# Hybrid convolution, attention and feed-forward kernel on Trainium2: the mean of the first feed-forward block's output is taken out by an fp16 matmul where the output is added, in place of an fp32 centring in the norm behind it

## What is computed

```
x = conv_block(x, L0); x = conv_block(x, L1)       # pointwise 24->96, depthwise 3x3, pointwise 96->24, shortcut
t = tokens(x)
t = t + linear_attention(_ln_t(t))
t = t + quantised_ffn(_ln_t(t), L2)                # fp8 products, fp16 sums
t = t + fourier_block(_ln_t(t))                    # FFT over the tokens, scale, ReLU, inverse FFT
t = t + quantised_ffn(_ln_t(t), L3)

def _ln_t(v, eps=1e-05):
    m = jnp.mean(v, axis=-1, keepdims=True)
    s = jnp.var(v, axis=-1, keepdims=True)
    return (v - m) / jnp.sqrt(s + eps)

def _qlinear(x, W, b):
    y = q_acc(jnp.einsum('bsk,nk->bsn', q_mul(x), q_mul(W)))
    return q_acc(y + q_mul(b))
h = jax.nn.relu(_qlinear(x, W1, b1)); y = _qlinear(h, W2, b2)
```

## Time and profile before

| | us |
|---|---|
| median of 3 runs (lowest to highest) | 2623.15 (2612.8 to 2631.39) |
| the profiled execution | 2623.52 |
| its span, first to last instruction | 2621.4 |
| TensorE busy | 2183.9 |
| VectorE busy | 1927.7 |
| ScalarE busy | 1611.5 |
| mean granted TensorE clock, as a share of full speed | 0.874 |

### The profile page before, as it was taken

How to read it: one execution, slowest core, us unless ns; L and a number is a source line. 1 busy time by engine, 2 the same in 40 slices (tenths; PEclk the granted TensorE clock), 3 DMA queues, 4 the chain that set the end, 5 groups by cost and what they waited for, 6 DMA issues and landing times.

```text
span 2621.4 us, 49010 instructions
## 1 busy us (share of the span) xinstructions
PE 2183.9 (83%) x19776; PEld 1269.9 (48%) x19776; DVE 1927.7 (74%) x3744; ACT 1611.5 (61%) x2758; POOL 113.7 (4%) x290
## 2 busy tenths in 40 slices
PE   3677878998889888998889887998889988986865
PEld 1233334663446534664446534465346634662653
DVE  4886987897768795799858795885957988456153
ACT  3344457855677575765777565864867647757554
POOL 1000000000000000000000000000000000000000
PEclk9887989998789898999889896996889988976665
DMA  5001001000020001000010002000010000000000
GB/s 137 1 1 19 1 1 20 2 2 1 1 38 2 1 1 35 4 2 1 4 35 2 2 1 38 1 2 1 1 30 2 2 1 1 20 2 1 20 1 19
DMA packets 108592, 29.69 MB, mean 11 GB/s; under 512 B 104144, under 2 KB 104272, under 8 KB 107984
## 3 DMA queue, kind: packets, MB, share of 16 engines
q1 hardware_dynamic: 108368, 26.56, 5.0%
HBM read 16.91 MB, written 9.63 MB: 10 GB/s over the span
## 4 chain that ended last, share of the span: by engine, by line
DVE 41%; PE 38%; ACT 11%; issue 6%; SPq 3%; DMA 1%; ACTq 0%; DVEq 0%
DVE acc L1475 20%; PE P L745 6%; PE P L726 5%; PE P L945 4%; PE P L1037 3%; SPq L586 3%; DVE SQ L1621 3%; PE P L794 3%; PE P L958 2%; PE P L986 2%; DVE arena L1605 2%; DVE T L1491 2%; PE P L767 1%; DVE T L1635 1%; PE P L1000 1%
## 5 line engine op out<-in xcount | busy, mean ns | idle before, releaser
L1475 DVE SCALAR_TENSOR_TENSOR acc<-H,Dm,acc 128x784 f32<-128x784 f32 x1024 | 989.4, 1027 | 74.1 <-ACT acc L1113 73.6
L726 PE MATMUL P<-T,Wk 112*128 112x448 f32 (+1 forms) x768 | 393.5, 605 | 77.3 <-ACT H L1106 37.7
L745 PE MATMUL P<-H,diag 64*64 64x392 f32 x4608 | 404.6, 501 | 18.4 <-DVE T L1491 18.4
L1106 ACT ACTIVATE H<-P,biasA 128x448 f32<-128x448 f32 (+1 forms) x384 | 236.0, 622 | 250.5 <-PE P L726 159.9
L745 PEld LDWEIGHTS P<-H,diag 64*64 64x64 f32 x4608 | 172.2, 135 | 234.0 <-issue 203.7
L726 PEld LDWEIGHTS P<-T,Wk 112*128 112x128 f32 x768 | 131.5, 203 | 201.5 <-ACT H L1106 103.3
L1136 ACT ACTIVATE acc<-P,biasT 128x392 f32<-128x392 f32 x128 | 68.6, 584 | 185.5 <-PE P L745 185.5
L794 PE MATMUL P<-T,pack_b 112*112 112x448 f32 x224 | 125.1, 655 | 15.0 <-DVE T L1580 7.9
L1491 DVE SCALAR_TENSOR_TENSOR T<-P,bias,T 112x392 f32<-112x392 f32 x128 | 77.2, 621 | 73.0 <-PE P L767 72.7
L970 PE MATMUL P<-pack_b,arena 128*96 128x112 f32 x928 | 111.5, 269 | 22.8 <-DVE roots L1621 11.7
L1113 ACT ACTIVATE acc<-H,Dm 128x784 f32<-128x784 f32 x128 | 121.9, 952 | 13.6 <-PE P L767 11.4
(11 more groups left out here) (205 smaller groups left out, 3766.8 us busy)
## 6 DMA issues: line engine op xcount, KB each, us to landing
xin<-in_x SPq DMA_DIRECT2D x224, 42.0 KB, 2.3
out_y<-arena SPq DMA_DIRECT2D x8, 1176.0 KB, 6.0
pack_b<-in_pack_b SPq DMA_DIRECT2D x1, 3926.5 KB, 18.0
arena<-in_pack_s SPq DMA_DIRECT2D x1, 1584.0 KB, 8.8
pack_a<-in_pack_a SPq DMA_DIRECT2D x1, 1084.0 KB, 5.4
pack_i<-in_pack_i SPq DMA_DIRECT2D x1, 320.0 KB, 3.1
arena<-in_pack_k SPq DMA_DIRECT2D x1, 192.0 KB, 3.3
```

What stands on the lines that cost most here:

```text
L726: pe.matmul(conv_rows(slice(0, 128), HB[(NP * s + e) % len(HB)], n), Wk1[:, 128 * j:128 * (j + 1)], image_rows(T[q % 3], a, n), start=True ...
L745: last = pe.matmul(conv_rows(slice(64 * h, 64 * (h + 1)), CVB + r, HH), diag[64 * r:64 * (r + 1), tap, :], H1[64 * r:64 * (r + 1), slot(s, ...
L1106: act.activation(H1[:, slot(s, j), o:o + n, 1:1 + HW], conv_rows(slice(0, 128), HB[(NP * s + e) % len(HB)], n), ACT.Relu, bias=biasA[:, j, ...
L1475: ins = ve.scalar_tensor_tensor(a, H1[:, slot(s, j), r:r + SR, c:c + HW], Dm[:, j, tap:tap + 1], a, ALU.mult, ALU.add)
```

## The change

In norm 2 the fp32 centring and the copy back are gone; ScalarE squares a chunk as soon as the feed-forward's add of it is done. In the first feed-forward, the biased fp16 output goes through one more matmul, fp16, with a 112 x 112 matrix `cen16` (24 times the centring matrix, so that its entries are whole numbers), into the output bank that the second layer has used; VectorE then adds 1/24 of that PSUM result to T in place of the fp16 tile. The output bank is free for the next chunk after this add, where it was free after ScalarE's copy. The add of chunk c stands one chunk later in the order than its bias. Norm 2 needs no bank, no `cenk` matrix and no semaphores for centring. The bare steps without an instruction that norms 1 and 3 had on TensorE are gone too. All turn strings are written anew (except that the shape of the order is as before: convolutions of quad q beside the middle of q - 1 and the back of q - 2).

```
-        "b3 m4 b3 m4 b1 m2 b2 m3 b2 m1 b176 "
+        "b130 "
...
+        cen16 = sb("cen16", [R, R], F16)
...
+        free_psum = sig("mean_free_ffn_out_in_psum", NCK)
...
-                    yield
-                    if i == 0:
-                        pe.wait_ge(written.sem, written.at(q, 2 * NS + rows_added(c) if n == 0 else c + 1))
+                    if n == 0:
+                        yield
+                        pe.wait_ge(written.sem, written.at(q, 2 * NS + rows_added(c)))
                         if c >= NC:
                             pe.wait_ge(norm.d_ready.sem, norm.d_ready.at(q, c - NC + 1))
-                        pe.matmul(P[0:R, cen[c % NC], 0:CK], par["cen" if n == 0 else "cenk"][0:R, :],
+                        pe.matmul(P[0:R, cen[c % NC], 0:CK], par["cen"][0:R, :],
...
-                        pe.wait_ge(f.out_half.sem, f.out_half.at(q, c - len(ob) + 1))
+                        read = f.added if L == 0 else f.out_half
+                        pe.wait_ge(read.sem, read.at(q, c - len(ob) + 1))
...
+                def mean_free(c):
+                    pe.wait_ge(f.out_biased.sem, f.out_biased.at(q, c + 1))
+                    stand(pe)
+                    pe.matmul(P[0:R, ob[c % len(ob)], 0:CK], cen16[:, :], f.o16[:, 1, c % 2, :],
+                              start=True, stop=True).then_inc(free_psum.sem, 1)
 
                 for c in range(NCK):
                     for j in range(NT):
                         v = NT * c + j
+                        if L == 0 and c >= 2 and j == 1:
+                            yield
+                            mean_free(c - 2)
                         yield
...
+                if L == 0:
+                    yield
+                    mean_free(NCK - 2)
                 yield
                 second(NCK - 1)
+                if L == 0:
+                    yield
+                    mean_free(NCK - 1)
...
-                    if i == 0:
+                    if n == 0:
                         act.wait_ge(norm.cen_psum.sem, norm.cen_psum.at(q, c + 1))
                         act.activation(D, P[0:R, cen[c % NC], 0:CK], ACT.Copy).then_inc(norm.d_ready.sem, 1)
                         act.wait_ge(norm.d_ready.sem, norm.d_ready.at(q, c + 1))
                     elif n == 1:
                         act.wait_ge(at_added.sem, at_added.at(q, c + 1))
+                    elif n == 2:
+                        act.wait_ge(ffns[0].added.sem, ffns[0].added.at(q, c + 1))
...
+                ve.tensor_scalar(cen16[:, :], par["cen"][0:R, :], float(CH), None, ALU.mult)
...
-                def out_add(c):
+                def out_bias(c):
                     ve.wait_ge(f.out_half.sem, f.out_half.at(q, c + 1))
                     ve.tensor_scalar(f.o16[:, 1, c % 2, :], f.o16[:, 0, c % 2, :], qb[L][0:R, NT:NT + 1], None, ALU.add).then_inc(f.out_biased.sem, 1)
-                    ve.wait_ge(f.out_biased.sem, f.out_biased.at(q, c + 1))
+
+                def out_add(c):
                     t = T[q % 3][:, CK * c:CK * (c + 1)]
-                    ve.tensor_tensor(t, t, f.o16[:, 1, c % 2, :], ALU.add).then_inc(f.added.sem, 1)
+                    if L == 0:
+                        ve.wait_ge(free_psum.sem, free_psum.at(q, c + 1))
+                        last = ve.scalar_tensor_tensor(t, P[0:R, ob[c % len(ob)], 0:CK], 1.0 / CH, t, ALU.mult, ALU.add)
+                    else:
+                        ve.wait_ge(f.out_biased.sem, f.out_biased.at(q, c + 1))
+                        last = ve.tensor_tensor(t, t, f.o16[:, 1, c % 2, :], ALU.add)
+                    last.then_inc(f.added.sem, 1)
...
+                    if c >= 2 and L == 0:
+                        yield
+                        out_add(c - 2)
                     if c >= 1:
                         yield
-                        out_add(c - 1)
-                yield
+                        out_bias(c - 1)
+                        if L == 1:
+                            out_add(c - 1)
...
-    c["cenk"] = c["cen"] + np.diag((np.arange(R) >= MR) & (np.arange(R) < PAD))
```

More of the change, by code:

```diff
@@ L74 @@
              ("w1", (NT * 128,)), ("b1", (NT,)), ("w2", (NT, R)), ("b2", (1,)))],
-    "b": [("cen", (R,)), ("cenk", (R,)), ("rest", (RC,)), ("sgn", (1,)), ("selv", (32 + (NCK - 1) * QI,)), ("m97", (RC + 1,)),
+    "b": [("cen", (R,)), ("rest", (RC,)), ("sgn", (1,)), ("selv", (32 + (NCK - 1) * QI,)), ("m97", (RC + 1,)),
           ("s97", (RC,)), ("wva", (CH,)), ("wkbd", (RC,)), ("bk", (1,)), ("wqt", (CH + 1,)),
@@ L86 @@
     "gpsimd": (
-        "d7 b1 c10 m1 c1 m1 c5 m1 c4 b2 c2 m2 c4 b2 c1 m1 c4 b2 m1 c1 m1 c3 b1 c1 b1 m1 c4 b2 c1 m1 c1 m1 c4 "
-        "b2 c1 m1 c4 b2 m1 c1 m1 c4 b2 c2 m1 c3 b2 c1 m2 c4 b2 m1 c3 b1 c1 b1 m1 c2 m1 c4 b2 c1 m1 c3 b2 m3 "
-        "b5 "
[3 rows of a table added]
     ),
     "tensor": (
[46 rows of a table removed]
[47 rows of a table added]
     ),
     "scalar": (
[37 rows of a table removed]
[38 rows of a table added]
     ),
     "vector": (
[23 rows of a table removed]
[30 rows of a table added]
     ),
@@ L474, in build @@
         for half, norm, layers in (("middle", normM, 2), ("back", normB, 2)):
-            norm.cen_psum = sig(f"centered_in_psum_{half}", NCK)
-            norm.d_ready = sig(f"centered_ready_{half}", NCK)
             norm.sq_ready = sig(f"squares_ready_{half}", layers * NCK)
@@ L484, in build @@
             norm.y_ready = sig(f"normalised_ready_{half}", layers * NCK)
+        normM.cen_psum = sig("centered_in_psum", NCK)
+        normM.d_ready = sig("centered_ready", NCK)
+        free_psum = sig("mean_free_ffn_out_in_psum", NCK)
         ones_ready = sig("yt_ones_ready", 2)
@@ L1043, in back @@
             def back(q):
-                yield from layer_norm(q, normB, 2, ffns[0].added)
+                yield from layer_norm(q, normB, 2)
                 yield from fourier(q)
@@ L1573, in ffn @@
                 f = ffns[L]
-                def out_add(c):
+                _, ob = ffn_banks(q, L)
+                def out_bias(c):
                     ve.wait_ge(f.out_half.sem, f.out_half.at(q, c + 1))
                     ve.tensor_scalar(f.o16[:, 1, c % 2, :], f.o16[:, 0, c % 2, :], qb[L][0:R, NT:NT + 1], None, ALU.add).then_inc(f.out_biased.sem, 1)
-                    ve.wait_ge(f.out_biased.sem, f.out_biased.at(q, c + 1))
+                def out_add(c):
                     t = T[q % 3][:, CK * c:CK * (c + 1)]
-                    ve.tensor_tensor(t, t, f.o16[:, 1, c % 2, :], ALU.add).then_inc(f.added.sem, 1)
+                    if L == 0:
[5 more added lines that the diff above has]
+                    last.then_inc(f.added.sem, 1)
                 for c in range(NCK):
@@ L1590, in ffn @@
                     last.then_inc(f.biased.sem, 1)
+                    if c >= 2 and L == 0:
+                        yield
+                        out_add(c - 2)
                     if c >= 1:
                         yield
-                        out_add(c - 1)
+                        out_bias(c - 1)
+                        if L == 1:
+                            out_add(c - 1)
+                if L == 0:
+                    yield
+                    out_add(NCK - 2)
                 yield
+                out_bias(NCK - 1)
+                if L == 0:
+                    yield
                 out_add(NCK - 1)
```

## The result

The changed kernel takes 2444.7 us (median of 4 runs, 2441.9 to 2448.8); the kernel before takes 2619.2 us on the same chip (4 runs). The profiled execution of the changed kernel took 2448.8 us, its span is 2447.0 us, and the mean granted clock rose from 0.874 to 0.903.

The account below looks back on a forecast made before the run. No engine was taken as full; a chain of waits changing engine bounds the kernel. Span 2621.4 - 17 (steady part) - 20 (end) = 2584.4, with 2.1 around it 2586.5, put to the median 2586; stated 2585, range 2565 to 2605.

Parts of the forecast that it names:

- The new orders themselves: All engines' rewritten step lists: may cost or give some 10 us, widening the range; not given a chance as a case.
- the steady part: Quads 0 to 6: 0 to 39 us less, 20 taken, less VectorE's 3 us: 17 us gained.
- the end: Behind the last convolution: quad 7's deviation 14.4 us after quad 6's last add instead of 28.9; 20 us gained (14 to 26).
- The price of a centring: Norm behind the feed-forward: removing centring frees 5.3 us of TensorE and 3.8 us of ScalarE per quad.
- The fp16 pass and the add: First feed-forward: each pass 0.3 us (range 0.19 to 0.35); VectorE's add from PSUM 0.05 us dearer, 3 us in all.
- The gap: Between one quad's convolution and the next, 1300 to 1340 us: 5.6 us of the chain are centring that the change removes.
- The router some 3 us sooner behind the last input piece: Sign of being right, in the gaps between quads: no centring on the chain, so the router's work starts earlier.
- The single output bank: Rival, middle's feed-forward, quads 0 to 6: bank held until the add, 1.4 us more per chunk, 69 us, 2655; chance 0.1.
- The clock: Rival, seven gaps: without dense fp32 passes the lower clock level lasts 10 us longer each, 35 us lost, 2621; chance 0.1.
- Only the end gains: Rival: input loads and the round trip take the gap's freed time; steady part nothing, end 14 us, 2612; chance 0.2.
- more than forecast: Rival: every gap gives its 5.6 us and the end 26 us, 2561; chance 0.12.
- as dear as fp32: Rival, first feed-forward: fp16 matmul costs as much as an fp32 one, so 25 us come back, 2611; chance 0.03.

Follow-up runs that it names:

- fp32_new_order: The kernel before with its fp32 centring and waits kept, but the changed kernel's step orders on all engines: 2482.7 us, ratio 0.947.
- experiment 1: Two kernels against the kernel before: old arithmetic in the new orders, 2482.7 us (0.947); new arithmetic in the old orders, 2726.6 us (1.040).

## Why the prediction was wrong

The step that failed is the sentence "The new orders themselves, which move every step a little, may cost or give some 10 us beside all this; that widens the range and is no case of its own." The orders alone gave 138 us in place of 10. No row stood behind the 10. That the steps move little is so: counted in the lists, 2.4 places in the mean on VectorE and 3.2 on TensorE, at most 27 and 28; that little movement makes little difference was assumed. The trace of the kernel before had what was at stake: VectorE idle for 413 us of the stretch, 147 of them in front of the taps and of the convolutions' output adds. The orders alone took away 109 of the 413 and 89 of the 147, with the same work on VectorE (1928.3 us busy, before 1927.7).

**The forecast for the rest agrees with the arithmetic's measured worth by luck.** Forecast -37, measured -38 on the new orders. It was split as 17 in the steady part and 20 at the end; from `fp32_new_order` to the changed kernel it is 34.9 in the stretch and 3.2 at the end. The forecast's 20 at the end were mainly the new list's, which gave 27.6 there; both together 30.8. So the term for the steady part was half of what was measured, and the term for the end, by its own reasoning mostly order, stands in for the rest.

**The price of a centring.** The forecast counted 5.3 us of TensorE and 3.8 us of ScalarE a quad. Over eight quads that is 73 us of work, of which 45 are seen in the time, 28 and 17.5. In the steady part the change came to 35, near the upper end of 0 to 39. That end was built on 5.6 us in each of seven gaps; but 2.2 of the 5.6 were norm 0's (above), and the gap was the longest of the seven, so that the reading at the gap would have given 7 x 3.4 = 24 at most. The gain lies in other places as well.

**The fp16 pass and the add.** The pass takes 352 ns at least and 368 at the median; 0.3 was taken, from a range to 0.35, so it lies just above that range. The add from PSUM was to be 0.05 us dearer than the one in SBUF and is not: 618 ns against a median of 626. Two lines by source, min/median/max:

```profile
L916 PE MATMUL P<-mid,cen x56: 352/368/622, 373.2 to 2272.7; 112*112 112x448 f16 x56
...
L1614 DVE SCALAR_TENSOR_TENSOR T<-P,T x56: 610/618/626, 377.1 to 2273.4; 112x448 f32<-112x448 f32 x56
```

**The gap.** "The router some 3 us sooner behind the last input piece" is wrong at the gap shown, 15.2 us against 14.5, though the gap is 20 us shorter. **The end.** Quad 6's output matmuls stand where it was forecast; the deviation comes behind quad 6's last add 18.1 us, forecast 14.4, because the last two chunks need 4.7 us from the output matmuls' end to the last add (2269.30 to 2274.0) where one pass and one add were counted.

**The single output bank** was a true mechanism with a price that was too low, and its condition was missing. In orders that were not made for it, it turns the change into a loss: the held bank costs 102/49 = 2.1 us a chunk, over the 0.76 from which it decides and over the 1.4 that was priced (the whole fp16 way 135/49 = 2.8). In the new orders TensorE waits 12.2 us for it in all. Why: the lists put other matmuls between a chunk's hidden layer and the second layer behind it, so that the bank is free, or nearly so, when its turn comes (experiment 1).

**The clock.** As a loss of the changed kernel it is out: 0.874 before, 0.906 with the new orders, 0.903 with the arithmetic as well. How much of the orders' 138 us is the higher clock's (the same instructions keep TensorE busy for 58 us less) and how much it only follows from the shorter waits is not separated. In the gap's slice with the input load it is 0.83 where it was 0.63. In the old orders the new arithmetic does lower it, to 0.843, together with the longer waits; how much of that kernel's 106 us is the clock's is not separated. The rule of the Trainium skill, "TensorE: Matmul & The Clock Gate", section "A second HAM failure mode: psum-queue depth-cycling", describes such a fall in a kernel whose matmul groups go from bank to bank with short idle times between them. The kernel in the old orders is in line with it, with 42 waits of 2.4 us in the mean and the clock at 0.843, though no run tells these waits from other causes; the changed kernel, with 20 waits of 0.6 us, shows no such fall.

**The other rivals.** "Only the end gains" is wrong, since the stretch gives 35 us for the arithmetic alone; "more than forecast" is wrong in its mechanism, since the change's surplus is the orders'; the pass is not as dear as fp32.

**What stays open.** It is shown that the orders make the difference, that the gain comes in every period, and, for the held bank, which wait the old orders make long. It is not shown which steps of the new orders give the 138 us of the old arithmetic: the new list might have been planned with better costs, or the old one be an unlucky one, and every mixture adds seams of its own. No experiment here took single steps.

## What to carry to other kernels

Where each engine works through a written list, a change of arithmetic that comes with a new list is two changes: price the list by the idle time that the engines have now, and measure the old arithmetic on the new list before you credit either. Do not judge a new data dependency (here a bank held for two more steps) on the old list alone: the same edit gave +4% there and -1.5% on a list written for it. Where an engine waits for the result of its own last step by way of two others, look whether its list has other work in between. Read fullness in slices of 15 us, since a mean of 75% can be an engine that is full and starved by turns. And where a view names no releaser for a wait, look at what ended just before it: here more than half of the wait for the bank stood under "issue".

## What was not expected of the hardware

A scaled add of 112 x 448 fp32 that reads PSUM and SBUF took 618 ns, no more than the plain one from SBUF alone (626), while the attention's, with a scale per partition, took 682. The fp16 pass over 448 columns takes 352 to 368 ns standing alone, as the fp8 one of 0.35 us, and 56 of them with all that hangs on them cost 7 us of 2445 in the new orders, which is hardly clear of noise.
